# Two phases of a vision tower made one: the feed-forward's weights rounded inside the attention phase, its last outputs made inside the feed-forward

## The reference

```python
h = tok(x)                                  # convolution, softmax attention
h = h + gated_attention(layernorm(h))
h = h + experts(layernorm(h))               # top 2 of 8, then a layernorm
h = h + l1_attention(layernorm(h))          # linear attention
h = h + bit_ffn(layernorm(h))
# l1_attention, for each image and head: q, k divided by their L1 norm over the tokens
kv = einsum('bhnd,bhne->bhde', k, v);  out = einsum('bhnd,bhde->bhne', q, kv) @ w_proj.T + b
# bit_ffn: weights rounded to -1, 0, 1 times mean(abs(w)); activations rounded to 8 bits by row
up, gate = split(bitlinear(x, w_in, g_in)); return bitlinear(silu(gate) * up, w_out, g_out)
# bitlinear: rmsnorm, quantise the rows, quantise the weights, multiply
```

## Time and profile before

| | |
|---|---|
| time, median of 3 runs | 2737.93 us (2736.9 to 2740.74) |
| profiled execution | 2735.24 us, its span 2733.4 us |
| busy share of the span | PE 84%, DVE 72%, ACT 57%, POOL 37% |
| mean granted TensorE clock | 0.893 of full speed |
| feed-forward's first input product | starts at 2308.82 us |

### The profile page before, as it was taken

One profiled execution on the slowest core, in us unless ns is written; L12 is line 12 of the kernel. 1 busy time (PEld: TensorE's weight loads), 2 busy tenths in 40 slices (PEclk: granted clock), 3 DMA queues, 4 the chain that ended last, 5 costly groups with the idle time before them and its releaser, 6 DMA issues. The chain is left out here.

```text
span 2733.4 us, 45420 instructions
## 1 busy us (share of the span) xinstructions
PE 2284.4 (84%) x14046; PEld 1656.8 (61%) x14047; DVE 1972.9 (72%) x5409; ACT 1553.5 (57%) x2693; POOL 1019.6 (37%) x1052
## 2 busy tenths in 40 slices
PE   8999999999996999999938999926778785666655
PEld 4444444444444888888827999916566683444444
DVE  5777777777773898888834444447698877888996
ACT  2444444444444788888735565536566551777776
POOL 1100100100000366666653444478686710344443
PEclk9999999999997999999958999957688887677787
DMA  2000000000003233333336777721111100000000
GB/s 57 0 18 13 0 18 13 0 9 1 0 0 95 33 68 72 74 71 74 74 124 219 255 257 254 237 74 50 45 49 43 47 8 23 21 26 21 26 26 26
DMA packets 82135, 172.44 MB, mean 63 GB/s; under 512 B 13425, under 2 KB 45334, under 8 KB 81694
## 3 DMA queue, kind: packets, MB, share of 16 engines
q1 hardware_dynamic: 39426, 94.27, 10.6%
q0 software_dynamic: 34496, 54.62, 8.7%
q10 hardware_dynamic: 8064, 21.68, 2.6%
HBM read 63.98 MB, written 63.88 MB: 47 GB/s over the span
## 5 line engine op out<-in xcount | busy, mean ns | idle before, releaser
L211 ACT ACTIVATE prob<-pscore 128x896 f32<-128x896 f32 x336 | 308.2, 917 | 422.9 <-PE pscore L293 422.9
L418 DVE TENSOR_REDUCE pmax<-ppre 112x1 f32<-112x512 f32 x656 | 424.4, 686 | 162.0 <-PE ppre L260 162.0
L307 PE MATMUL pout<-prob,xkey 128*64 128x448 f32 x1344 | 327.9, 566 | 0.4 <-ACT prob L211 0.4
L260 PE MATMUL ppre<-xh,yh 49*112 49x512 f32 x656 | 291.2, 446 | 7.8 <-DVE pmax L418 4.2
L193 POOL CAST yh<-ynext 113x448 fp32r<-113x448 f32 x28 | 17.2, 614 | 667.4 <-DVE pmax L418 639.2
L723 POOL DMA_INDIRECT rows_in<-xr,idx x224 | 223.3, 997 | 111.7 <-issue 59.6
L260 PEld LDWEIGHTS ppre<-xh,yh 49*112 49x112 f32 x656 | 112.6, 172 | 239.4 <-issue 103.5
L1710 POOL DMA_INDIRECT yg<-rows_out,place x224 | 228.2, 1019 | 62.4 <-issue 62.2
L293 PE MATMUL pscore<-yh,xh 49*128 49x448 f32 x700 | 241.0, 422 | 0.4 <-DVE yh L438 0.4
L2225 POOL TENSOR_TENSOR yg<-y,gout 112x512 f32<-112x512 f32 x112 | 141.1, 1270 | 259.1 <-DVE y L2458 259.1
L1560 POOL TENSOR_TENSOR zl<-z,zh 128x448 fp32r<-128x448 f32 x126 | 144.5, 1147 | 217.0 <-ACT zh L1526 207.5
(11 more groups left out here) (388 smaller groups left out, 6563.3 us busy)
## 6 DMA issues: line engine op xcount, KB each, us to landing
wd<-down SPq DMA_DIRECT2D x63, 512.0 KB, 3.0
xb<-rows_in SPq DMA_DIRECT2D x63, 448.0 KB, 3.6
rows_out<-yb ACTq DMA_DIRECT2D x63, 336.0 KB, 3.2
h<-brow POOLq DMA_DIRECT2D x28, 336.0 KB, 5.2
out<-ho SPq DMA_DIRECT2D x28, 336.0 KB, 2.8
rows_in<-zero SPq DMA_DIRECT2D x15, 448.0 KB, 5.9
rows_in<-xr,idx POOLq DMA_INDIRECT x224, 2.8
yg<-rows_out,place POOLq DMA_INDIRECT x224
```

Of the source, the lines that this page charges most:

```text
L211: nc.scalar.activation(prob[j % 3][:, :, :], pscore[j % 2][:, :, 0:CH], ACT.Exp).then_inc(exped, 1)
L260: pe.matmul(out[:, :], yh1[rows, q * T:(q + 1) * T], xh[b % 2][rows, block * 512:(block + 1) * 512], start=True, stop=True, tile_position= ...
L307: mm = pe.matmul(pout[i * LO:(i + 1) * LO, 0:CH], xkey[b % 2][:, 2 * j + i, :], prob[j % 3][:, i, :], start=(j == 0), stop=(i == 1 and j = ...
L418: nc.vector.reduce_max(pmax[:, q, 2 * block + half:2 * block + half + 1], bank(u, depth), AX.X).then_inc(pre_max, 1)
```

## The change

The two phases become one, attention_and_ffn_phase. finish_stats for the last layer and bit_ffn_phase go; their work is taken in as follows.

- SP starts the gains' transfers at the phase's start and the weights' when the last chunk's experts have been added (they lie in the buffers of the gathered rows; other feed-forward tiles lie in attention tiles too).
- VectorE sums the weights after step 25 (sum_weights), makes the statistics of the first 64 tiles and rounds the weights after step 26 (finish(0), round_weights), and weighs and quantises chunk 0 after step 27. TensorE's part of the sums, weights_summed, comes after its q_and_k of step 25.
- fac is made by a power on POOL, for 64 tiles and, in chunk 7, for 48. 1/root, its root on ScalarE and the refinement on VectorE are gone. The variance's two constants are folded into one scaling.
- The last nine chunks' outputs are made by halves, all in bank 0 of po (map_late, add_half), since the feed-forward's product out uses bank 1. The two of the third image stay beside the map's chain. The seven of the fourth are put into feed-forward chunks 0 to 6, two halves each.
- transpose_in(0) stands right after turn_gram, ahead of the map's chain, and enter(0) after image_map. In the loop transpose_in(g + 1) comes after into(g, 2) instead of ahead of it, since its bank is now shared with transpose_y.
- ScalarE's table is set for Silu at the start of the phase instead of for Abs.

```diff
+            sp.dma_start(gin[:], ins["gin5"]).then_inc(F["gin_in"], 16)
+            sp.dma_start(gout[:], ins["gout5"]).then_inc(F["gin_in"], 16)
+            sp.wait_ge(S["acc_out"], NC)
+            sp.dma_start(win, ins["win5"]).then_inc(F["w_in"], 16)
+            sp.dma_start(wout, ins["wout5"]).then_inc(F["w_in"], 16)
...
+            def factor5(n, cols):                                        # POOL
+                pool.wait_ge(F["fac_in"], n + 1)
+                nc.gpsimd.tensor_tensor(fac[:, cols], var[:, cols], mhalf5[:, cols], ALU.pow).then_inc(F["fac_out"], 1)
+            factor5(0, slice(0, HEAD))
+            pool.wait_ge(F["gin_in"], 32)
+            for g in range(NC):
+                weigh(g, 0)
+                weigh(g, 1)
+                root_of(g)
+                if g == AFTER:
+                    factor5(1, slice(HEAD, NT))
...
+            def map_late(n, r):                                          # TensorE
+                pe.wait_ge(S["h_out"], 2 * n + r + 2)
+                map_half(n, r, 0)
+            def weights_summed():
+                pe.wait_ge(F["set"], 2)
+                pe.wait_ge(F["wc"], 1)
+                pe.wait_ge(S["h_out"], 2 * (NC - 2 - LATE) + 2)
+                pe.matmul(po[:, 0, 448:449], ones[:], wsum[:, 0:1], start=True, stop=True, skip_group_check=True)
+                pe.matmul(po[:, 1, 448:449], ones[:], wsum[:, 1:2], start=True, stop=True,
+                          skip_group_check=True).then_inc(F["wsum_mm"], 1)
...
                 q_and_k(s, b, c)
+                if s == NC - 3:
+                    weights_summed()
             turn_gram(B - 1)
-            map_out(NC - LATE)
+            transpose_in(0)
+            map_late(NC - LATE, 0)
+            map_late(NC - LATE, 1)
             keys_map(B - 1)
-            map_out(NC - LATE + 1)
+            map_late(NC - LATE + 1, 0)
             values_map(B - 1)
             project_map(B - 1)
+            map_late(NC - LATE + 1, 1)
             image_map(B - 1)
-            for n in range(NC - LATE + 2, NC):
-                map_out(n)
+            enter(0)
+            for g in range(NC):
+                if g:
+                    transpose_y(g - 1)
+                into(g, 2)
+                if g + 1 < NC:
+                    transpose_in(g + 1)
+                into(g, 3)
+                if g < CPI:
+                    map_late(NC - CPI + g, 0)
+                if g:
+                    outof(g - 1, 0)
+                if g < CPI:
+                    map_late(NC - CPI + g, 1)
+                if g:
+                    outof(g - 1, 1)
+                if g + 1 < NC:
+                    enter(g + 1)
...
-            nc.scalar.preload_act_table(ACT.Abs)
+            nc.scalar.preload_act_table(ACT.Silu)
...
+            def finish(n, cols):                                         # VectorE
+                nc.vector.tensor_tensor(mean[:, cols], bns[:, cols, 1], bns[:, cols, 4], ALU.add)
...
+                nc.vector.tensor_scalar(var[:, cols], var[:, cols], (1 + 1e-6) / D, 1e-11, ALU.mult,
+                                        ALU.add).then_inc(F["fac_in"], 1)
+                dve.wait_ge(F["fac_in"], n + 1)
...
+                if s == NC - 3:
+                    sum_weights()
+                if s == NC - 2:
+                    finish(0, slice(0, HEAD))
+                    round_weights()
+                if s == NC - 1:
+                    dve.wait_ge(F["gin_in"], 32)
+                    weigh_in(0)
+                    largest_in(0)
+                    quant_in(0)
             gram_turned(B - 1)
-            add_out(NC - LATE)
+            add_half(NC - LATE, 0, 0)
+            add_half(NC - LATE, 1, 0)
...
                 gated(g, 3)
+                if g < CPI:
+                    add_half(NC - CPI + g, 0, 0)
+                if g == CPI:
+                    dve.wait_ge(S["h_out"], 2 * NC + 2)
+                    stats_of(NT - 2)
                 if g:
                     result(g - 1, 0)
                 mean_square(g)
                 largest_y(g, 1)
+                if g < CPI:
+                    add_half(NC - CPI + g, 1, 0)
                 if g:
                     result(g - 1, 1)
                 quant_y(g)
+                if g == AFTER:
+                    finish(1, slice(HEAD, NT))
```

More of the change, by code:

```diff
@@ L1364, in expert_phases @@
                        held + route_sems)
-        linear_attention_phase(nc, ins, h, bns, rstd, minus, eye, gate, place, rows_out)
+        attention_and_ffn_phase(nc, ins, h, bns, mean, rstd, var, minus, eye, gate, place, rows_out, out)
 def tile_phase(nc, ins, eye, down, slot, place, shift, tile_e, tile_r, rows_in, rows_out, held):
@@ L1619, in _, with attention_and_ffn_phase @@
             take_y(NTILE - 1, (NTILE - 1) % 2, (NTILE - 1) // 2)
-def linear_attention_phase(nc, ins, h, bns, rstd, minus, eye, gate, place, rows_out):
+def attention_and_ffn_phase(nc, ins, h, bns, mean, rstd, var, minus, eye, gate, place, rows_out, out):
+    HID = 512
+    MAGIC = 12582912.0
+    HEAD = 16 * TPC
     RB = D - 128
@@ new lines, in transpose_in @@
+            def transpose_in(g):
+                if g:
+                    pe.wait_ge(F["yT_out"], 2 * g - 2)
+                else:
+                    pe.wait_ge(S["xT_out"], NC)
+                    pe.wait_ge(S["xL_out"], NC)
+                pe.wait_ge(F["xq_out"], g + 1)
+                for q in range(TPC):
+                    for c in range(2):
+                        mm = pe.transpose(pxt[:, c, q * T:(q + 1) * T], xq[:, q, c * KC:(c + 1) * KC], eyeb[0:T, 0:T])
+                mm.then_inc(F["xtr_mm"], 1)
@@ new lines, in enter, with outof @@
+            def enter(g):
+                pe.wait_ge(F["xT_out"], g + 1)
+                if g == 0:
+                    pe.wait_ge(F["ready"], 3)
+                    pe.wait_ge(S["a_sum"], 2 * NC)
+                    pe.wait_ge(S["g_out"], B)
+                into(g, 0)
+                if g == 0:
+                    pe.wait_ge(S["wi_out"], B)
+                into(g, 1)
+            def outof(g, pair):
+                if 2 * g + pair:
+                    pe.wait_ge(F["o_out"], 2 * g + pair)
+                pe.wait_ge(F["yT_out"], 2 * g + 2)
+                for i in range(2):
+                    q = 2 * pair + i
+                    for k in range(4):
+                        mm = pe.matmul(po[0:T, 1, i * D:(i + 1) * D], yT[:, k, q * T:(q + 1) * T], woutq[:, k, :],
+                                       start=(k == 0), stop=(k == 3), skip_group_check=True)
+                mm.then_inc(F["o_mm"], 1)
@@ new lines, in result @@
+            def result(g, pair):
+                if pair == 0 and g:
+                    dve.wait_ge(F["stored"], 16 * g)
+                dve.wait_ge(F["d2_out"], g + 1)
+                dve.wait_ge(F["o_mm"], 2 * g + pair + 1)
+                for i in range(2):
+                    q = 2 * pair + i
+                    st = nc.vector.scalar_tensor_tensor(ho[:, q, :], po[0:T, 1, i * D:(i + 1) * D], d2[:, q:q + 1],
+                                                        h[:, g * TPC + q, :], ALU.mult, ALU.add)
+                st.then_inc(F["o_out"], 1)
```

664 lines of the change are left out of this document (298 added, 366 removed).

## The result

The changed kernel takes 2747.86 us (median of 6, 2743.3 to 2751.16) against 2738.93 for the kernel before beside it (median of 6): a ratio of 1.0035, 95% interval 1.0025 to 1.0045. It is slower by some 9 us where 12 us less were forecast. The two profiled executions, 2746.98 and 2735.24 us, have spans of 2745.2 and 2733.4.

A forecast was written before the change was run, and what follows sets the result against it. Bound: VectorE in the chunks; in the seam TensorE's outputs, then VectorE's serial work. -33.1 (mark) + 17.5 + 2.7 + 1 = -12 us from 2735.24 gives 2723, or 2726 against the median; range 2718 to 2732, extended to 2750.

The forecast's parts named there:

- Step 25: Seam: VectorE sums the weights after its step sum; TensorE's next transposes wait to about 2232.4, +4.9 us.
- step 27: Seam: ten matmuls and last sum, 2.8 us, to 2254.3; weighing, largest and quantisation add 5.0, to 2259.3.
- the mark's rest: Mark: start of VectorE's second input quantisation, 2309.01 before; chunk 1's weighing and largest, 2.4 us, put it at 2275.9.
- The clock: Step 26: after a new TensorE idle stretch part runs at the lower clock level, 1.7 us (0 to 9.4).
- Map chain: Last image's map on TensorE, late halves sharing one bank: 14.2 us (13.8 to 16.2) against 13.8 before.
- The order of input matmuls and transposes: Other chunks: new order costs 0, as the first input matmul waits for its gate anyway (-3 to +3 over 28).
- First seven chunks: Each takes over two half-chunks of output: 2.5 us (1.65 to 4), seven cost 17.5 us (11.6 to 28).
- After the seventh: Statistics of the last two tiles and finish(1) between two chunks on VectorE: 2.7 us (2 to 2.7).
- the power on POOL: Replaces ScalarE's root and VectorE's refinement; 1 us taken for both uses (bound 24).
- The power holds VectorE: Rival: VectorE waits behind finish(0) and finish(1), 0.2 us a column, 24 us in place of 1; 2749 us, chance 0.35.
- The moved outputs cost what they cost before: Rival: low clock meets the moved halves, early chunks grow 4 us each, 28 in all; 2737 us, chance 0.20.
- low(27) after 2258: Sign of a wrong forecast: VectorE's low(27) in the seam, expected near 2251, ends later than 2258.

The follow-up runs named there:

- e_warm2: Changed kernel with 59 unread matmuls of 384 columns, about as long as the waits, in TensorE's four waits ahead of and around the map chain: 2733.19 us, 0.9982.
- e_warm: Changed kernel with 130 small unread matmuls in TensorE's same four seam waits; they took some 41 us where the waits are 10.9: 2770.49 us, 1.0115.
- e_steady: Changed kernel with unread matmuls filling the four waits ahead of the map chain and two TensorE waits in each chunk: 2716.71 us, 0.993.
- e_order: Changed kernel with the next input's transposes moved behind the fourth input product: 2747.59 us, 1.0036.
- e_bank: Changed kernel with input transposes in po's free bank from chunk 8 on, ahead of the third input product as before the change: 2741.81 us, 1.0007.
- e_best2: e_best with the fourth image's seven outputs made in one go ahead of the first input product, in both banks: 2723.69 us, 0.995.
- e_best: Changed kernel with the edits of e_early and e_bank, and the second power cut into pieces of 4 columns: 2718.74 us, 0.9928.
- e_early: Changed kernel with weight statistics and sums in step 26, chunk 0's quantisation in step 27, rounding in pieces inside the map chain: 2726.07 us, 0.9951.
- the filled kernel before: Kernel before the change with unread matmuls in two TensorE waits of each chunk (rounded y, first result of the product out): 2728.46 us, 0.9976.
- e_hot: Changed kernel with 15 unread matmuls per chunk in TensorE's wait for the rounded y: 2740.02 us, 1.0017.

## Why the prediction was wrong

*Step 25, step 27, the mark's rest*: right within 1.4 us by the stamps, in part by luck. *The clock* (1.7 us, 0 to 9.4): from step 26's transposes to step 27's it took 13.0 us (2230.71 to 2243.72), and 8.7 in e_warm2 (2238.65 to 2247.32), so the term was 4.3, inside its bounds but 2.6 more than taken. The stamps hide it because this execution came to step 25's sum 1.5 us earlier than the one before; from the end of that sum to the transposes it took 4.1 us where 4.4 were forecast.

*Map chain* (14.2 us, 13.8 to 16.2): this step failed, by 9.5 us (23.7 measured). The prediction took the earlier trace rows's 13.8 us at a clock of 1.00 and gave the new waits, of step 27 and of transpose_in(0), no effect on it, though it had read the same effect off for step 26. Its upper bound left out the one thing that the step before had named. What the runs showed in its place is a chain at 0.50 from end to end. At 1.00 the chain took 13.4 us (e_warm, e_warm2, e_steady), better than forecast.

*The order of input matmuls and transposes* (0, -3 to +3), and with it the late chunks priced as unchanged: failed, by 13.5 us. "The first input matmul waits for its gate anyway" was true and beside the point, since it is the fourth product that came late. And its size depends on the clock: 0.0 us at 1.00 (14.24 in both kernels), 0.6 at 0.77 (15.10 against 14.52), and what the alternation adds. The order is not the whole of it: without the gate's wait (e_order) the chunks took 15.29, with the old order (e_bank) 15.05, against 14.58 before. What carries the loss is the clock in the loop, since with both waits filled the means are 14.33 and 14.37; which of the edits lets the loop settle in the slower patterns stays open. The way in which the loop is entered, the rival in e_bank's expectation, finds no support: in e_warm2, whose chain ran at 1.00, these chunks took 15.37 as in the changed kernel, and in e_best2, without late halves in the loop, 14.97 against 15.04 in e_best. The late chunk of the earlier trace rows stood for all, though the kernel before has late chunks of 14.3 to 15.3 us at clocks from 0.65 to 0.88; a period that moves with the clock should have got bounds from these, not from gates.

*First seven chunks* (2.5 each): right, 16.2 for seven in the trace; at 1.00 they take 16.67 against 14.24, 2.4 each. *After the seventh* and *the power on POOL*: their sum of 3.7 is the trace's 3.6, but not by the working: the power cost some 2.5 to 3 us once, where gains stood behind it, and nothing on its first use.

*The power holds VectorE* came to 2749, next to the time measured, by chance, and is refuted. Its price per column was near (10.55 us for 64 columns, 8.02 for 48: some 0.165 each), its mechanism wasn't: beside the first power VectorE's rounding took its ordinary 1.28 us, and in e_early, where the power ran from 2233.32 to 2243.86, the weighing with two inputs from the on-chip memory took 1.40 us from 2239.10 on, the same as alone:

```profile
2233.32 10.54 POOL L1823 TENSOR_TENSOR fac<-var,mhalf 112x64 f32<-112x64 f32 x1 [6.07 <-DVE var L2422]
...
2239.10 1.40 DVE L2430 SCALAR_TENSOR_TENSOR xg<-h,mean,gin 112x192 f32<-112x192 f32 x4
```

The mean square's row, which spoke for the rival, comes again in the changed kernel (2606.76 for 0.59 us, ending with POOL's gain at 2607.3), so a scaling does end late beside POOL's gain. Beside its second power the same kind of scaling took an ordinary 0.17 us (2424.39). The Trainium skill, SBUF — State Buffer, section Who interferes with whom, would have the second of the two wait for the whole instruction; in these runs it doesn't hold for the power, and the measurement decides.

*The moved outputs cost what they cost before* is refuted in its place, for the early chunks took 16.2 to 17.8 us and not 18.5; but the low clock that it feared cost as much elsewhere. Neither sign by which the forecast was to be known as wrong appeared (low(27) after 2258, early chunks over 18.5): both watched terms that held.

The two failures have one root: the forecast priced the change at a steady high clock. With the clock held (e_steady against the filled kernel before) the difference is -11.8 by medians and -7.9 by traces, where -12 was forecast, and the mark falls at 2275.55 where 2275.9 was.

## What to carry to other kernels

In this seam a wait put on TensorE was paid twice, once as idle time and once as what followed at half the clock: when a step adds waits of 1 to 3 us, price every stretch behind them at both levels, not the next one alone. This loop, in which TensorE idles some 4 to 6 us of a chunk, has no single period, and a chunk's mean clock does not give it either (14.52 us at 0.76 and 15.30 at 0.78 in the kernel before, 14.53 at 0.85 and 16.18 at 0.82 in e_hot). To learn what an order costs by itself, hold the clock in both kernels. Work that is moved beside a busy phase should be cut to fit the idle stretches there: the same instructions, placed so that TensorE waited less, were worth 22 us.

## What the runs showed of the hardware

- The clock fell behind short waits: in e_early TensorE waited 1.26 us just ahead of the chain and 0.72 and 0.63 us in it, and the level still went to 0.50 at 2259.3. In e_warm2 it stayed at 1.00 with waits of 0.95, 0.71 and 0.51 us there, so the waits' lengths alone don't tell.
- Being busy did not always raise it. In e_warm TensorE ran matmuls of 64 columns without a gap for 21 us at 0.50, while a later filling of the same matmuls, begun at 1.00, kept 1.00 for 6.8 us. The changed kernel's chain was busy for 22.36 of 23.58 us and stayed at 0.50. The filling with 384 columns stayed at 1.00 or rose to it. The Trainium skill, TensorE: Matmul & The Clock Gate, section What's actually happening, says that activity releases the lower level; the 21 us don't agree with that, and the measurement decides.
- The loop settles in patterns by itself: 0.56 and 0.78 in turn in e_order, 0.82 and 0.85 in e_hot, in both over more than ten chunks.
- POOL's power took 10.55 us for 64 columns, 8.02 for 48 and 1.01 for 4: some 0.16 us for each further column.
